# Eight post-layernorm layers on one core: the start of the window attention inside the ternary layer, bias rows in bf16, moved splits and sums, a last chunk by tiles

## The reference

```python
def _L0_ffn_ref(x, weight, bias):            # l0f
    return x @ (sign(weight) * mean_abs(weight)).T + bias
# l1: attention of 16 heads on one key and value head, + bo;  l1f: Hadamard GLU
def _L2_attn_ref(x, ...):                    # l2, segments of 256 rows
    u, v = x @ Wu.T + bu, x @ Wv.T + bv
    gates = sigmoid(relu(x @ Wg1.T + bg1) @ Wg2.T + bg2)
    return conv3(x) + (cumsum(u * gates) * (v * gates)) @ Wu
def _L2_ffn_ref(x, W_fc, W_proj):            # l2f
    h = square(relu(x @ ternary(W_fc).T))
    return rms_norm(h) @ ternary(W_proj).T
def _L3_attn_ref(h, ...):                    # l3, window of 64, 16 heads of 128
    q = rmsnorm(rope(h @ wq_comp @ wq_up), q_norm_w)
    k = rmsnorm(rope(h @ wk), k_norm_w);  v = h @ wv
    probs = softmax([q k' / sqrt(128) in the window, sink_logit])
    return concat((probs @ v) @ out_w1[group]) @ out_w2
def _L3_ffn_ref(x, ...):                     # l3f
    return (silu(x @ Wg.T) * (x @ Wu.T)) @ Wd.T
```

## Time and profile before

| | us |
|---|---|
| median of 3 runs | 1732.24 (1724.12 to 1732.43) |
| the profiled execution | 1730.56 |
| its span on the core | 1728.7 |
| PE busy in it | 1624.0 (94%) |
| DVE, ACT, POOL busy | 1038.1 (60%), 790.5 (46%), 366.9 (21%) |
| mean granted PE clock | 0.969 of full speed |

### The profile page before, as it was taken

The page is one execution under the profiler, slowest core; times in us unless marked ns, Lnnn a source line. Parts: engine busy times, 40 slices in busy tenths (PEclk is TensorE's granted clock), DMA queues, the critical chain, the costliest instruction groups (busy, mean ns, idle before and its releaser), DMA issues.

```text
span 1728.7 us, 25533 instructions
## 1 busy us (share of the span) xinstructions
PE 1624.0 (94%) x9844; PEld 972.9 (56%) x9852; DVE 1038.1 (60%) x1867; ACT 790.5 (46%) x1797; POOL 366.9 (21%) x420
## 2 busy tenths in 40 slices
PE   7999879999999999999999889977999999999998
PEld 4666544433333334454566456765777777774556
DVE  4666577787787774533534774316777777952222
ACT  3331335657667776622111143316677767642110
POOL 2321000000100000400000023404555555640000
PEclk9999879999999999999999989987999999999999
DMA  5000220000000002010000030000000020000000
GB/s 179 2 2 21 60 75 2 2 1 2 1 1 2 1 1 77 27 50 0 16 0 0 1 118 5 1 6 1 8 1 7 1 83 2 2 1 0 13 13 25
DMA packets 28362, 34.98 MB, mean 20 GB/s; under 512 B 5713, under 2 KB 24722, under 8 KB 27730
## 3 DMA queue, kind: packets, MB, share of 16 engines
...
...
## 4 chain that ended last, share of the span: by engine, by line
PE 82%; DVE 11%; ACT 3%; issue 3%; POOL 1%; DMA 0%; POOLq 0%; SPq 0%; DVEq 0%; ACTq 0%
PE PS L1157 8%; PE PS L1144 7%; PE PS L1116 7%; PE PS L1408 6%; PE PS L1414 6%; PE PS L2495 6%; PE PS L1436 6%; DVE arena L1325 4%; PE PS L2108 3%; PE PS L2484 3%; PE PS L2462 3%; PE PS L2078 2%; PE PS L339 2%; PE PS L2438 2%; PE PS L1193 2%
## 5 line engine op out<-in xcount | busy, mean ns | idle before, releaser
L1247 ACT ACTIVATE arena<-PS 128x512 f32<-128x512 f32 (+3 forms) x640 | 319.7, 534 | 175.9 <-PE PS L1144 77.7
L1325 DVE TENSOR_REDUCE arena<-PS 128x1 f32<-128x1024 f32 (+7 forms) x320 | 329.8, 1061 | 97.6 <-PE PS L1118 69.7
L1144 PE MATMUL PS<-arena 99*128 99x512 bf16 (+3 forms) x640 | 205.8, 353 | 1.4 <-ACT arena L1247 1.0
L1116 PE MATMUL PS<-arena 96*128 96x512 bf16 (+3 forms) x640 | 179.0, 358 | 18.3 <-DVE arena L1325 17.5
L1157 PE MATMUL PS<-arena 128*32 128x512 f32 (+3 forms) x1280 | 150.5, 542 | 2.8 <-ACT arena L1253 1.7
L190 POOL TENSOR_TENSOR rstd<-ve,mhalf 128x4 f32<-128x4 f32 x32 | 32.3, 1010 | 535.8 <-DVE ve L218 535.7
L1144 PEld LDWEIGHTS PS<-arena 99*128 99x128 bf16 x640 | 60.7, 99 | 147.4 <-ACT arena L1247 115.9
L185 ACT ACTIVATE XT<-PS 128x1024 f32<-128x1024 f32 x32 | 32.8, 1024 | 225.1 <-PE PS L178 225.1
L2603 ACT ACTIVATE arena<-arena 128x128 f32<-128x128 f32 x256 | 122.7, 484 | 1.3 <-DVE arena L2782 1.3
L2495 PE MATMUL PS<-arena 128*128 128x256 f32 x512 | 121.0, 379 | 0.2
L1408 PE MATMUL PS<-XT,arena 128*128 128x512 f32 x256 | 120.4, 592 | 0.1
(11 more groups left out here) (241 smaller groups left out, 2779.2 us busy)
## 6 DMA issues: line engine op xcount, KB each, us to landing
...
```

What stands on the lines that cost most here:

```text
L1116: last = pe.matmul(flat[:, o:o + w], q, a.KS[0:SROWS, CH * kc:CH * kc + w], start=True, stop=kc < c)
L1144: last = pe.matmul(PS[:, b, lo:CH], a.KS[0:rows, P * j:P * (j + 1)], a.QS[0:rows, G1 * g + r, CH * c + lo:CH * (c + 1)], start=True, stop= ...
L1247: act.activation(a.PB[:, n % 3, r, lo:CH], PS[:, 4 + x % 3, lo:CH], ACT.Exp, scale=D0 ** -0.5).then_inc(a.e2, 1)
L1325: dve.tensor_reduce(dst, src, AX.X, ALU.max, negate=True).then_inc(a.m1, 1)
```

## The change

1. **l0f's bias.** The bias is loaded to three partitions. `l0f_bias_parts` (eight DVE instructions on three partitions, at n = 12 of l0's loop) splits it into three bf16 parts that add up to it, one a row, and a bf16 product of three rows of ones takes the place of the fp32 product with one row.
2. **End of l0f, start of l1 on DVE.** The last norm of the chunk list stands ahead of `l1_low` of chunk 0, and low and the first residual of chunk 1 ahead of `l1_keys`. The last chunk's residual stands ahead of the step loop, its low part at the third step and its keys at the fourth.
3. **l2.** u's product is a function of its own (`l2_u_pe`); that of chunk 1's second half stands ahead of the transposes of the last GLU chunk. `l2_sums` of the next but one chunk stands in DVE's wait for POOL in each tail.
4. **l2 to l2f.** The relus and hidden squares of the first tiles stand between the splits of x; the last chunk's `tail_act` comes behind them; the last two chunks' middle, high, residual and low parts go into l2f's first chunks.
5. **l3's front.** The keys, compress and the first four projections stand between the `down` of l2f's last chunk, in banks 0 to 3 (`FRONT3`), four of the eight W12 pairs (banks 0 to 3) with the turns of the keys and of the first tile's queries behind the last `down`, ahead of l2f's last transposes, which go to banks 4 and 5. W12 pairs 4 to 7 stand in l3's first groups. ACT, DVE and POOL have their parts of it at the matching places; `squares` of the last chunk comes one `down` earlier.
6. **Last chunk of l3f.** Each tile has a PSUM bank of its own, and is summed, normed and stored by itself (128 KB). The transposes and copies of the last layer, which nobody reads, are left out.
7. Three unused semaphores go, and the row factors of l2f lie elsewhere.

The diff, cut to its core (functions of l3 that were only moved out of their parents are left out):

```diff
         if n == 8:
             l0f_signs(k, dve, st)
+        if n == 12:
+            l0f_bias_parts(k, dve, st)
...
-    sp.dma_start(a.bias[0:1, :], I["L0_ffn_bias"].partition_broadcast(1)).then_inc(a.ld, 16)
+    sp.dma_start(a.bias[0:3, :], I["L0_ffn_bias"].partition_broadcast(3)).then_inc(a.ld, 16)
...
+def l0f_bias_parts(k, dve, st):
+    a = k.l0f
+    dve.wait_ge(a.ld, 32)
+    dve.wait_ge(k.l0.ldx, 16 * 6)
+    b, r, high, rows = a.bias[0:3, :], k.R[0:3, 0, :], k.R[0:3, 1, :].bitcast(BF16)[:, 0:E], a.bparts[0:3, :]
+    chosen = lambda p: k.ident[0:3, p:p + 1]
+    dve.memset(a.onesb[0:3, :], 1.0)
+    st.link(dve.tensor_copy(high, b))
+    st.link(dve.tensor_tensor(r, b, high, ALU.subtract))
+    st.link(dve.tensor_scalar(rows, high, chosen(0), None, ALU.mult))
+    st.link(dve.tensor_copy(high, r))
+    st.link(dve.tensor_tensor(r, r, high, ALU.subtract))
+    st.link(dve.scalar_tensor_tensor(rows, high, chosen(1), rows, ALU.mult, ALU.add))
+    dve.scalar_tensor_tensor(rows, r, chosen(2), rows, ALU.mult, ALU.add).then_inc(a.bias_s, 1)
...
-        pe.matmul(F, k.ones[0:1, :], a.bias[0:1, :], start=True, stop=False)
+        pe.matmul(F, a.onesb[0:3, :], a.bparts[0:3, :], start=True, stop=False)
...
-            l1_low(k, dve, 0)
-    normed(len(EARLY) - 1)
+            normed(len(EARLY) - 1)
+    l1_low(k, dve, 0)
+    l1_residual(k, dve, 1, 0)
     l1_keys(k, dve, st, 0)
-    l1_residual(k, dve, 1, 0)
     l1_residual(k, dve, 1, 1)
...
+    l1_residual(k, dve, LAST1, 0)
     for n in P1.steps:
         if n in P1.mt_at:
             maxima_rows(P1.mt_at[n])
+        if n == FIRST1 + 2:
+            l1_low(k, dve, LAST1)
+        if n == FIRST1 + 3:
+            l1_keys(k, dve, st, LAST1)
...
-            l1_residual(k, dve, LAST1, 0)
-            l1_low(k, dve, LAST1)
-            l1_keys(k, dve, st, LAST1)
...
+                F = k.PS[:, F_BANK + j, 0:E] if s == LAST and c == NC - 1 else f_tile(k, j)
+                last = pe.matmul(F, a.h[:, c % 2, it, P * j:P * (j + 1)], a.down[:, it, :],
...
-        if c >= 1:
+        if c >= 1 and s < LAST:
...
+def last_tiles_dve(k, dve, st):
+    F = k.PS[:, F_BANK:F_BANK + TPC, 0:E]
+    X = k.X[:, TPC * (NC - 1):TPC * NC, :]
+    def norm(j):
+        dve.wait_ge(k.tile_rstd, j + 1)
+        dve.tensor_scalar(X[:, j, :], k.R[:, j, :], k.mv[:, j, 0:1], k.rstd[:, j:j + 1], ALU.subtract, ALU.mult)\
+           .then_inc(k.tile_normed, 1)
+    dve.wait_ge(k.xn_done, NC * (LAST + 1) - 1)
+    for j in range(TPC):
+        dve.wait_ge(k.tile_out, j + 1)
+        st.link(dve.tensor_tensor(k.R[:, j, :], F[:, j, :], X[:, j, :], ALU.add))
+        st.link(dve.bn_stats(k.stats[:, j, :], k.R[:, j, :]))
+        st.link(dve.bn_aggr(k.mv[:, j, :], k.stats[:, j, :]))
+        dve.tensor_scalar(k.ve[:, j:j + 1], k.mv[:, j, 1:2], LN_EPS, None, ALU.add).then_inc(k.tile_ve, 1)
+        if j >= 1:
+            norm(j - 1)
+    norm(TPC - 1)
...
     if j == TPC:
         l2_hidden_pe(k, pe, 1)
+        l2_u_pe(k, pe, 1, 0)
         l2_gates_pe(k, pe, 1, 0)
+        l2_u_pe(k, pe, 1, 1)
...
-    for c in (NC - 2, NC - 1):
-        if c == NC - 1:
-            for n in range(2):
-                l2f_relu(k, act, n)
-        tail_act(k, act, NC * 5 + c, c)
-        act.wait_ge(k.xt_done, NC * 4 + c + 1)
-        x_middle(k, act, c - 1)
-        x_high(k, act, c)
+    tail_act(k, act, NC * 6 - 2, NC - 2)
+    act.wait_ge(k.xt_done, NC * 5 - 1)
+    l2f_relu(k, act, 0)
+    x_middle(k, act, NC - 3)
+    l2f_relu(k, act, 1)
+    x_high(k, act, NC - 2)
+    tail_act(k, act, NC * 6 - 1, NC - 1)
...
-            for r in range(KT):
-                l2_sums(k, dve, st, c + 1, r)
-                l2_gated(k, dve, c + 1, r)
+            l2_gated(k, dve, c + 1, 0)
+            l2_sums(k, dve, st, c + 1, 1)
+            l2_gated(k, dve, c + 1, 1)
             l2_conv(k, dve, st, c + 1)
         tail_sum(k, dve, NC * 4 + c, c)
         tail_stats(k, dve, st, NC * 4 + c)
+        if c + 2 < NC:
+            l2_sums(k, dve, st, c + 2, 0)
         if c == NC - 1:
             l2f_hidden(k, dve, 0)
         tail_norm(k, dve, NC * 4 + c, c)
         dve.wait_ge(k.xn_done, NC * 4 + c + 1)
+        if c == NC - 1:
+            l2f_hidden(k, dve, 1)
         if c >= 2:
             x_low(k, dve, c - 2)
+        if c == NC - 1:
+            l2f_hidden(k, dve, 2)
         if c >= 1:
             x_residual(k, dve, c - 1)
...
-            if d == TPC:
+            if d == (TPC if c + 1 < NC else 3):
...
+            if c + 1 == NC:
+                l3_front_pe(k, pe, d)
+        if 1 <= c < NC - 1:
             tail_pe(k, pe, NC * 6 + c - 1, c - 1)
-    tail_pe(k, pe, NC * 7 - 1, NC - 1)
...
+            if (c, it) == (0, 4):
+                x_middle(k, act, NC - 2)
+            if (c, it) == (0, 6):
+                act.wait_ge(k.xt_done, NC * 5)
+                x_high(k, act, NC - 1)
+            if (c, it) == (1, HT - 1):
+                x_middle(k, act, NC - 1)
...
+            if (c, it) == (1, 2):
+                x_low(k, dve, NC - 2)
+            if (c, it) == (1, 5):
+                x_residual(k, dve, NC - 1)
...
+        if c + 1 == NC:
+            mean(c)
+            l3_front_dve(k, dve, st)
+        dve.wait_ge(a.rms, c + 1)
+        tail_dve(k, dve, st, NC * 5 + c, c, row_scale=a.rs)
         if c == 0:
             x_low(k, dve, NC - 1)
...
+FRONT3 = {("kv", 0): 0, ("qc", 0): 2, ("project", 0, 0): 2, ("project", 0, 1): 0, ("project", 1, 0): 2, ("project", 1, 1): 0}
...
+def l3_front_pe(k, pe, d):
+    a = k.l3
+    if d == 0:
+        pe.wait_ge(a.ld, L3_LOADS)
+        pe.wait_ge(k.l2f.r_s, HT * NC)
+        l3_keys(k, pe, 0)
+    if d == 1:
+        l3_compress(k, pe, 0)
+    if d == 3:
+        pe.wait_ge(k.l2f.ms, NC)
+        pe.wait_ge(a.b6, L3_USES["qc", 0][0])
+        l3_project(k, pe, 0, 0)
+    if d == 4:
+        l3_front_free(k, pe, ("kv", 0))
+        l3_project(k, pe, 0, 1)
+    if d == 5:
+        tail_pe(k, pe, NC * 7 - 2, NC - 2)
+        l3_front_free(k, pe, ("project", 0, 0))
+        l3_project(k, pe, 1, 0)
+    if d == 6:
+        l3_front_free(k, pe, ("project", 0, 1))
+        l3_project(k, pe, 1, 1)
+    if d == 7:
+        pe.wait_ge(k.xt_done, NC * 6 - 1)
+        l3_turn_keys(k, pe, 0)
+        l3_front_free(k, pe, ("project", 1, 1))
+        l3_w12(k, pe, 0)
+        l3_w12(k, pe, 1)
+        pe.wait_ge(a.q_add, 1)
+        l3_front_free(k, pe, ("ktr", 0))
+        l3_turn(k, pe, 0, 0)
+        l3_w12(k, pe, 2)
+        l3_w12(k, pe, 3)
+        pe.wait_ge(a.q_add, 2)
+        l3_front_free(k, pe, ("turn", 0, 0))
+        l3_turn(k, pe, 0, 1)
+        tail_pe(k, pe, NC * 7 - 1, NC - 1, F_BANK)
...
+    pe.wait_ge(a.w12_ev, 4)
     scores(0)
+    pe.wait_ge(k.xt_done, NC * 6)
+    l3_w12(k, pe, 4)
+    l3_w12(k, pe, 5)
     for n in range(NG3 + 3):
         t, g = n // GT3, n % GT3
         c, j = t // TPC, t % TPC
         if n + 1 < NG3:
             scores(n + 1)
+        if n < 2:
+            l3_w12(k, pe, 6 + n)
...
+def l3_front_act(k, act):
+    a = k.l3
+    act.wait_ge(k.l2f.add_s, ADDS2 * NC)
+    act.wait_ge(k.l2f.h_s, HT * NC)
+    l3_keys_in(k, act, 0)
+    l3_compressed(k, act, 0)
+    l3_projected(k, act, 0, 0)
+    l3_key_squares(k, act, 0)
+    l3_projected(k, act, 0, 1)
+    tail_act(k, act, NC * 7 - 2, NC - 2)
+    l3_projected(k, act, 1, 0)
+    l3_projected(k, act, 1, 1)
+    act.wait_ge(k.f_ready, NC * 6)
+    act.wait_ge(a.prep, 1)
+    l3_keys_out(k, act, 0)
+    l3_squares(k, act, 0)
+    l3_w12_out(k, act, 0)
+    l3_w12_out(k, act, 1)
+    l3_turned(k, act, 0, 0, 6, a.b6)
+    l3_turned(k, act, 0, 0, 7, a.b7)
+    l3_w12_out(k, act, 2)
+    l3_w12_out(k, act, 3)
+    l3_turned(k, act, 0, 1, 6, a.b6)
+    l3_turned(k, act, 0, 1, 7, a.b7)
+    tail_act(k, act, NC * 7 - 1, NC - 1, F_BANK)
...
+    l3_keys_add(k, pool, 0)
+    l3_keys_rms(k, pool, 0)
+    for half in range(2):
+        l3_add(k, pool, 0, half)
+    pool.wait_ge(k.f_ready, NC * 6)
...
+def l3_front_dve(k, dve, st):
+    l3_rotate_keys(k, dve, 0)
+    l3_keys_ms(k, dve, st, 0)
+    l3_keys_norm(k, dve, 0)
+    l3_rotate_queries(k, dve, 0)
...
-    rotate_keys(0)
-    rotate_queries(0)
-    keys_ms(0)
-    keys_norm(0)
+    queries_ms(0)
     rotate_queries(1)
...
+            for j in range(TPC):
+                t = TPC * (NC - 1) + j
+                sp.wait_ge(k.tile_normed, j + 1)
+                sp.dma_start(out[0, P * t:P * (t + 1), :], k.X[:, t, :]).then_inc(stored, 16)
```

399 lines of the change are left out of this document (222 added, 177 removed).

## The result

The changed kernel takes 1664.32 us (median of 4 runs, 1662.74 to 1665.95), the kernel before 1728.18 (4 runs, 1723.54 to 1732.43): a ratio of 0.9625, with a 95% interval of 0.9598 to 0.9653. That is 63.9 us by the medians. A second set on another occasion gave 1664.37 against 1728.46, 64.1 us, and the same ratio. The predicted 1669 was 4.7 too high and its range, 1652 to 1692, holds the result. The profiled execution of the changed kernel took 1662.74 us, 67.8 under that of before (1730.56), which itself lies 2.4 over the median of its kind.

What follows compares the result with a forecast made beforehand. PE was taken as the bound (82% of the chain), with waits and lower-clock work. Terms 6.7 + 5.4 + 2.5 + 14.2 + 29 + 4.2 = 62.0 off the profiled 1730.56 gave 1669 us, range 1652 to 1692.

Steps and rivals of the forecast that it cites:

- A: l0f's bias rows: the three-row bf16 product saves 0.42 us on each of sixteen tiles, 6.7 us (5.6 to 11.0).
- B: End of l0f: DVE's earlier norm and residual remove PE waits and some lower-clock time, 5.4 us (2.4 to 8.3).
- C: l1's first steps: DVE's new order saves its 1.5 us wait and about 1 of PE's catching up, 2.5 (1.5 to 5).
- E and F: l2 and l2f's first chunks: reordering removes 13.5 of 17.1 us PE waits plus lower-clock time, 14.2 us (10 to 17).
- G: l3's front inside l2f's last chunk: last down products to second compress falls from 94.4 to 65.5 us, saving 29 (22 to 33).
- H: Kernel's end: tile-by-tile finish saves 3.3 us and dropping unread transposes 0.87, together 4.2 us (3 to 5).
- lower level stays: Rival: PE's lower clock level (1.2 instead of 2.4 GHz) persists wherever it is now; gain about 42, 1689 us; chance 0.13.
- transposes: Rival: l3's new front, rich in transposes, is held at the lower clock level, losing 11 of G; 1680 us; chance 0.07.
- front waits in its new place: Rival: l3's front meets new in-order queue waits between down products, so G gives 20 only; 1678 us; chance 0.13.
- Slower: Rival: l0f and the new front drop wholly to the lower clock level, 1740 us; slower or no gain, chance 0.03.

## Why the prediction was right

The predicted sum was 62.0, the medians say 63.9 and 64.1. But the sum was made against the profiled execution of before, and between the two profiled executions it is 67.8, 5.8 more than predicted; that the medians come within 2 is in part luck. (The range's lower end of 1652 was 1 over the sum with all high ends, 1651; nothing hangs on it.) Part by part: A 6.7 (by the tiles' spacing), B 4.1 to 8.2, C 2.6 (means of eleven and of three), E and F 12.5 to 14.3, G 28.0 to 28.4, H 5.5, that is 59 to 66. The lower ends are those of the runs with a part undone. What they lack of the 67.8 is for the most part the lower level, which lasted longer in the trace of before than in these runs: 4.1 in B, 1.8 in E and F, both behind the same waits, and about 3 in C, where it is argued from the length of the low stretches and not measured.

- **A** was right in size. Its reason was nearly so: the price of few rows was put at 0.34 for one row, and as staying but for 0.07. It is 0.40 for one row and 0.30 for three. Of the prediction's two cases (5.6 if the price stays whole, 11.0 if it goes) the 6.7 lies near the first. The 0.34 was too low because 3.62 / 4 holds the end of the last product: from 144.32 to the next row of that trace, at 147.77, is 3.45, so a product takes 0.43 and not 0.45.
- **B** was put in the middle between no clock back (2.4) and all of it (8.3). All of it came back: the range was right, the choice low by 2.8. How much there is to come back varies: the old order costs 4.1, 7.5 and 8.2 in three traces.
- **C** was right against the mean (2.6 for 2.5), and in its mechanism: DVE's order saves some 2 us of PE's waiting. The other half of the 5.8 between the two first traces is the spread of this stretch, in which the lower level lasts 24 us after the change and 37 before.
- **E and F** were right in sum and wrong in both halves, so that the 14.2 for 14.3 is luck. I had 13.5 of the waits go and 3.6 stay; 7.5 went and 9.6 stayed. I had 3.7 of the clock come back and then took 3 off for the waits that stay; 6.8 came back. The step that failed in the waits is the hand-laid order. The longest wait that remains, 2.12 at 996.00, is for a relu that stands on ACT behind the last copy to XT, which waits for transposes that themselves wait 1.60 for the norm (992.79): I had taken the copy at the end of ACT's list for harmless. What I missed on the other side is the clock: behind these two waits it is at 0.53 for 3 us (996 to 999) and back at 1.00, where before it stayed low for 13.7 us in 1012 to 1048. I had also left out two shorter low stretches before, at 954 to 957.5 (0.51, behind the wait of 2.44) and at 1005.2 to 1008.8 (0.53, behind that of 1.90), some 7 us together, in which PE was busy throughout; both are gone.
- **G** was 1.0 too large. The last down and the front ended at 1108.4, 25.9 after the start, against 24.2. I had named the late end of the chain after that as DVE's and ACT's. That was wrong: PE is busy for 63.2 of the 67 us and waits for 3.2. The work at the full level came to 63, not 61.
- **H** was 1.3 too small: POOL takes 0.64 for one column and not 1.15, and from the last norm's start to the end is 2.5, where I had 0.4 and a store of 2.9, for which I had given no row. The 0.9 for the unread transposes was right.
- The rival in which the **lower level stays** (1689) is refuted: 0.992 mean, 1.00 in B's, l2's and G's stretches; only l1's first steps keep most of it. So is the one in which **transposes** hold the front at the lower level: 28 of them stand between 1108 and 1119 and the stretch is at 1.00. The sentence of TensorE: Matmul & The Clock Gate (Trainium skill, Part 4) that transposes don't count as busy in the same way is not borne out or refuted by that, since W12 products stand between them; it had no consequence here. The rival in which the **front waits in its new place** didn't come: the projections wait for nothing. **Slower** didn't come; l0f stayed at 1.00.
